# Moving batch 0's hand-over and the first two units' attention in among the last projections

## The reference

```
sa, ca, ga, sb, cb, gb = split(silu(c) @ wmod)         # per batch; ga, gb kept at least 0.25 from 0
h = layernorm(x) * (1 + ca) + sa
Q = elu(h Wq' + bq) + 1;  K = elu(h Wk' + bk) + 1;  V = h Wv' + bv
KV = sum over tokens of K (x) V, per head;  Ksum = sum over tokens of K
x = x + ga * ((Q KV / (Q . Ksum + 1e-6)) Wo' + bo)
h = layernorm(x) * (1 + cb) + sb
logits = cosine(h, centroids) + h . w_route;  gates = softmax over the two largest
x = x + gb * sum over experts of gate_e * (gelu(h w1_e + b1_e) w2_e + b2_e)
```

## Time and profile before

| | |
|---|---|
| median of 3 runs | 370.66 us |
| profiled execution | 370.4 us |
| its span | 368.6 us |
| TensorE matmul busy | 95% |
| VectorE, ScalarE, GpSimd busy | 80%, 63%, 71% |
| mean granted TensorE clock | 0.995 |

### The profile page before, as it was taken

The page is one execution under the profiler, slowest core; times in us unless marked ns, Lnnn a source line. Parts: engine busy times, 40 slices in busy tenths (PEclk is TensorE's granted clock), DMA queues, the critical chain, the costliest instruction groups (busy, mean ns, idle before and its releaser), DMA issues.

```text
span 368.6 us, 8941 instructions
## 1 busy us (share of the span) xinstructions
PE 348.6 (95%) x2762; PEld 324.9 (88%) x2762; DVE 294.4 (80%) x828; ACT 233.2 (63%) x510; POOL 263.2 (71%) x374
## 2 busy tenths in 40 slices
PE   7999999999997778699999999999999999999895
PEld 7877888888886677699999999999999999999895
DVE  4768777778776779989999898898988988887754
ACT  4476787787974475568384684674855856855541
POOL 3446999999886748887878889778778777666200
PEclk9999999999999899999999999999999999999999
DMA  7942630000000020341321323224214224224221
GB/s 271 331 143 66 202 108 0 0 0 2 1 2 0 2 93 31 110 126 56 109 86 60 129 59 105 88 70 131 86 58 142 79 65 130 94 68 138 83 69 57
DMA packets 23712, 31.78 MB, mean 86 GB/s; under 512 B 2288, under 2 KB 14204, under 8 KB 23680
## 3 DMA queue, kind: packets, MB, share of 16 engines
q1 hardware_dynamic: 23240, 31.34, 27.3%
q10 hardware_dynamic: 440, 0.04, 0.1%
HBM read 27.04 MB, written 4.34 MB: 85 GB/s over the span
## 4 chain that ended last, share of the span: by engine, by line
PE 78%; DVE 12%; issue 4%; ACT 3%; DMA 2%; POOL 1%; ACTq 0%; DVEq 0%; POOLq 0%
PE bank L777 22%; PE bank L779 20%; PE bank L778 20%; PE bank L785 5%; PE bank L844 2%; PE bank L815 2%; PE bank L956 2%; DMA g_bc<-in_b 1%; DVE hid_g L1357 1%; PE bank L882 1%; DVE den L1296 1%; PE bank L997 1%; DVE bank L1374 1%; PE bank L890 1%; DVE gT_f L1413 1%
## 5 line engine op out<-in xcount | busy, mean ns | idle before, releaser
L717 ACT ACTIVATE bank<-bank,cols_sb 128x256 f32<-128x256 f32 x128 | 51.3, 439 | 48.1 <-PE bank L779 47.7
L777 PE MATMUL bank<-tr_hi,w_hi 128*128 128x256 f32 x256 | 73.8, 288 | 0.0
L779 PE MATMUL bank<-tr_hi,w_lo 128*128 128x256 f32 x256 | 72.7, 284 | 0.0
L778 PE MATMUL bank<-tr_lo,w_hi 128*128 128x256 f32 x256 | 72.6, 283 | 0.0
L777 PE MATMUL bank<-w_hi,hid_pair 128*128 128x256 f32 x252 | 70.4, 280 | 0.1
L779 PE MATMUL bank<-w_hi,hid_pair 128*128 128x256 f32 x252 | 70.2, 279 | 0.0
L778 PE MATMUL bank<-w_lo,hid_pair 128*128 128x256 f32 x252 | 70.2, 278 | 0.0
L489 POOL TENSOR_TENSOR hid_pair<-hid_g,hid_pair 128x512 fp32r<-128x512 f32 x42 | 54.2, 1291 | 7.1 <-ACT hid_pair L724 3.9
L777 PEld LDWEIGHTS bank<-tr_hi,w_hi 128*128 128x128 f32 x256 | 48.9, 191 | 0.1
L779 PEld LDWEIGHTS bank<-tr_hi,w_lo 128*128 128x128 f32 x256 | 48.8, 191 | 0.0
L778 PEld LDWEIGHTS bank<-tr_lo,w_hi 128*128 128x128 f32 x256 | 48.8, 191 | 0.0
(11 more groups left out here) (159 smaller groups left out, 937.2 us busy)
## 6 DMA issues: line engine op xcount, KB each, us to landing
g_bc<-g_dram SPq DMA_DIRECT2D x64, 256.0 KB, 3.5
x_sb<-in_x SPq DMA_DIRECT2D x16, 256.0 KB, 3.3
out<-x_sb SPq DMA_DIRECT2D x15, 256.0 KB, 2.3
early<-in_wmod SPq DMA_DIRECT2D x3, 512.0 KB, 7.0
q_sb<-in_w SPq DMA_DIRECT2D x2, 512.0 KB, 6.4
q_sb<-in_w SPq DMA_DIRECT2D x1, 1024.0 KB, 9.4
mod_row<-mod_dram SPq DMA_DIRECT2D x1, 1024.0 KB, 6.2
q_sb<-in_wqkvT SPq DMA_DIRECT2D x2, 384.0 KB, 5.2
```

Source lines behind the costliest of these rows:

```text
L717: last = ac.activation(half, half, ACT.Gelu, bias=b1_sb[:, e:e + 1])
L777: te.matmul(out_ap, l_hi, r_hi, start=start, stop=False, skip_group_check=shared)
L778: te.matmul(out_ap, l_hi, r_lo, start=False, stop=False, skip_group_check=shared)
L779: return te.matmul(out_ap, l_lo, r_hi, start=False, stop=stop, skip_group_check=shared)
```

## The change

Batch 0's hand-over goes into steps 9 to 11 of phase A, the attention of units 0 and 1 and the norm of unit 0 into steps 10 to 15. The steps 8 to 15 are written out on all engines, and of the hand-written prologue only a few calls are left.

```diff
@@ TensorE, step_a
                 qk(u, 0)
+                if u.nth(NU - 1):
+                    attend(unit(1))
                 if u.plus(1) and not u.nth(0):
                     tp_a(u.plus(1))
+                if u.nth(UPB + 1):
+                    sum_k(0, bank[0][:, 0:E])
+                if u.nth(UPB + 2):
+                    make_m(0, bank[1])
+                if u.nth(UPB + 4):
+                    tp_o(unit(0))
+                if u.nth(UPB + 6):
+                    tp_o(unit(1))
                 qk(u, 1)
...
+                if u.nth(UPB + 5):
+                    attend(unit(0))
                 v(u)
@@ TensorE, step_e and what stands between the phases
+            def fill(to, n):
+                for _ in range(n):
+                    te.matmul(to[:, 0:E], ones_r[:, :], b2_r[:, :], start=True, stop=True)
...
+                if u.nth(1):
+                    first(u, 2)
                 if u.plus(3):
                     attend(u.plus(3))
-                if u and not u.nth(0):
+                if u and not early:
                     first(u, 2)
...
+                if u.nth(-1):
+                    pe.wait_ge(a_acc, NU + 1)
+                    fill(bank[6], 7)
                 if u.plus(2):
                     tp_e(u.plus(2))
+                if u.nth(-1):
+                    fill(bank[6], 11)
...
                     route(u.plus(2))
+                if u.nth(-1):
+                    sum_k(1, bank[6][:, 0:E])
+            pipeline(te, step_a, 2, 4, UPB)
+            tp_e(u0)
+            kv(unit(NU - 1))
             pe.wait_ge(route_ready, 1)
             route(u0)
@@ GpSimd, step_a (rstd_e(unit(0)) comes first in step UPB + 6)
+                if u.nth(UPB + 2):
+                    pool.wait_ge(f_ksrow, 1)
+                    gp.memset(prod[:, :, D:D + 1], DEN_EPS)
+                    make_prod(unit(0))
+                if u.nth(UPB + 3):
+                    make_qz(unit(0))
+                    make_prod(unit(1))
+                if u.nth(UPB + 4):
+                    make_qz(unit(1))
+                if u.nth(UPB + 6):
+                    make_prod(unit(2))
-                if u.plus(-2) and not u.plus(-2).nth(NU - 4) and not u.plus(-2).nth(NU - 3):
+                if u.plus(-2) and not any(u.nth(j) for j in range(UPB + 2, NU)):
                     add_bo(u.plus(-2))
@@ GpSimd, step_e
-                if any(u.nth(j) for j in range(2, 6)):
-                    add_bo(u.plus(NU - 6))
+                if u.plus(-2) and not any(u.nth(j) for j in range(UPB + 2, NU)):
+                    add_bo(u.plus(UPB - 2))
@@ ScalarE
+            def hi_m(b, product):
+                act.wait_ge(f_m_read, b + 1)
+                ac.activation(m_hi[:, b, :, :].rearrange("p c n -> p (c n)"), product[:, :], ACT.Copy).then_inc(f_m_hi, 1)
...
             def step_a(u):
+                if u.nth(UPB + 3):
+                    hi_m(0, bank[1])
                 negative_part(u, 0)
...
-                if u.plus(1) and cast_at_end(u.plus(1)):
+                if u.plus(1) and cast_late(u.plus(1)):
                     cast_activations(u.plus(1))
...
                 exp_qk(u, 1)
+                if u.nth(UPB + 6):
+                    normalise_e(unit(0))
+                if u.nth(UPB + 6):
+                    hi_o(unit(1))
                 if u.plus(2):
                     normalise(u.plus(2))
+                if u.nth(UPB + 4):
+                    hi_o(unit(0))
+                if u.nth(NU - 1):
+                    square(unit(0))
+                keep_v(u)
@@ VectorE, step_a, with mask_kv and split_m cut in two each (place_kv; scale_m and lo_m)
                 if u.plus(-2):
                     add_kv(u.plus(-2))
+                if u.nth(UPB + 3):
+                    denominators(unit(0))
+                if u.nth(UPB + 4):
+                    denominators(unit(1))
+                if u.nth(NU - 1):
+                    denominators(unit(2))
                 if not u.nth(0) and not u.nth(1):
                     split_weights(u)
...
                 feature_map(u, 0)
+                if u.nth(NU - 1):
+                    add_attention(unit(1))
                 feature_map(u, 1)
...
+                if u.nth(UPB + 1):
+                    keep_ksum(0, bank[0][:, 0:E])
+                    ve.memset(kv_m[:, :, :], 0.0)
+                    mask_kv(0)
+                    place_kv(0)
+                if u.nth(UPB + 2):
+                    scale_m(0, bank[1])
+                if u.nth(UPB + 3):
+                    lo_m(0, bank[1])
+                if u.nth(UPB + 4):
+                    lo_o(unit(0))
+                if u.nth(UPB + 5):
+                    add_attention(unit(0))
+                    stats_e(unit(0))
+                if u.nth(UPB + 6):
+                    lo_o(unit(1))
+                    modulate_e(unit(0))
+                if u.nth(NU - 1):
+                    stats_e(unit(1))
@@ VectorE, step_e (batch 1: place_kv in step 3 behind gates_b, scale_m at the end of step 3, lo_m in step 4)
-                if u.nth(-1):
-                    keep_ksum(1, bank[5][:, 0:E])
...
+                if u.nth(-1):
+                    keep_ksum(1, bank[6][:, 0:E])
```

More of the change, by code:

```diff
@@ L759, in step_e @@
                     hi_hid(u, 3)
-            pipeline(ac, step_a, 0, 2, NU - 4, NU - 1)
-            hi_o(u0)
-            step_a(unit(NU - 1))
-            hi_o(unit(1))
-            keep_v(unit(NU - 1))
-            normalise_e(u0)
-            square(u0)
+                if u.nth(3):
+                    hi_m(1, bank[7])
+            pipeline(ac, step_a, 0, 2, UPB)
             hi_e(u0)
@@ L791, in tp_a @@
                 wait(pe, a_xn, u.count(1, 1))
-                wait(pe, a_hf, u.count(1, -1))
-                if u.nth(NU - 2):
-                    pe.wait_ge(f_ksrow, 1)
-                if u.nth(NU - 1):
-                    pe.wait_ge(f_m_read, 1)
-                transposes(nat[:, u.h, :, :], bank[u.h]).then_inc(a_tp, 1)
+                wait(pe, a_hf, u.count(1, 0))
+                transposes(nat[:, 0, :, :], bank[5]).then_inc(a_tp, 1)
             def qk(u, t):
@@ L878, in _ @@
             for c in range(NC):
-                last = te.matmul(bank[5][:, 0:NE], ones_f, cent_sq[:, c, :], start=(c == 0), stop=(c == NC - 1))
+                last = te.matmul(bank[0][:, 0:NE], ones_f, cent_sq[:, c, :], start=(c == 0), stop=(c == NC - 1))
             last.then_inc(cent_done, 1)
@@ L911, in make_m @@
                 last.then_inc(f_m, 1)
-            pe.wait_ge(a_hf, NU - 3)
-            sum_k(0, bank[0][:, 0:E])
-            step_a(unit(NU - 3))
-            pe.wait_ge(d_wo, 16)
-            pe.wait_ge(a_hf, NU - 2)
-            make_m(0, bank[1])
             def tp_o(u):
@@ L946, in tp_e @@
                     wait(pe, o_x1, u.count(1, 2))
-                transposes(nat[:, u.h, :, :], bank[0]).then_inc(e_tp, 1)
+                transposes(nat[:, 1, :, :], bank[0]).then_inc(e_tp, 1)
             def route(u):
-                h = u.h
+                h = place_e(u)
                 wait(pe, e_lo, u.count(1, 1))
@@ L1058, in step_e @@
                     route(u.plus(2))
[L1060 to L1070 removed]
+                if u.nth(-1):
+                    sum_k(1, bank[6][:, 0:E])
+            pipeline(te, step_a, 2, 4, UPB)
+            tp_e(u0)
             kv(unit(NU - 1))
[L1072 to L1075 removed]
+            pe.wait_ge(b2_ready, 3)
             pe.wait_ge(route_ready, 1)
@@ L1475, in step_e @@
                 if u.nth(3):
-                    split_m(1, bank[7])
-            dve.wait_ge(mod_got, 16)
-            ve.memset(kv_m[:, :, :], 0.0)
-            keep_ksum(0, bank[0][:, 0:E])
-            mask_kv(0)
-            step_a(unit(NU - 3))
-            split_m(0, bank[1])
-            step_a(unit(NU - 2))
-            denominators(u0)
-            lo_o(u0)
-            denominators(unit(1))
-            add_kv(unit(NU - 3))
-            split_weights(unit(NU - 1))
-            dve.wait_ge(w_ready, NU)
@@ L1498, in _ @@
+            clip_centroids()
+            stats_a(unit(2))
+            split_b2()
+            split_route()
+            step_a(u0)
+            mod_rows(0)
+            bias_o()
+            step_a(unit(1))
+            mod_rows(1)
+            pipeline(ve, step_a, 2, 4, UPB)
             add_kv(unit(NU - 2))
-            modulate_e(u0)
-            add_attention(unit(1))
-            denominators(unit(2))
+            lo_e(u0)
             add_kv(unit(NU - 1))
-            lo_e(u0)
-            stats_e(unit(1))
```

278 lines of the change are left out of this document (118 added, 160 removed).

## The result

The kernel takes 367.06 us in the median after the change (366.38 to 369.39, 11 runs) and 370.58 us before it (367.74 to 371.76, 11 runs in turn with them): ratio 0.9922, 95% interval 0.9893 to 0.9951, so 3.5 us or 0.8% faster. The forecast was 367.0. The profiled execution took 367.11 us with a span of 365.0, the one before 370.4 with 368.6.

What follows compares the result with a forecast made beforehand. TensorE was taken as the bound, 95% busy, with VectorE late in the changeover. Terms -2.8 - 1.05 + 1.85 - 1.55 and 0.05 rounding gain 3.6 us: 366.8 from the profiled 370.4, 367.0 as median; range 363.7 to 371.0.

Steps and rivals of the forecast that it cites:

- Steps 8 to 14: End of the projections: seven steps of 41.5 us, plus 3.45 of added TensorE work and 1.45 of waits.
- The wait for split_lo(13): Step 12: GpSimd's added work makes TensorE wait 0.5 us for the low part of unit 13; bounds 0 and 1.3.
- ScalarE's 0.1: Steps 8 to 14: moving the activations' cast from VectorE to ScalarE costs 0.1 us; bounds 0 and 3.5 in all.
- make_m's wait as a cost: Step 10: TensorE waits 0.85 us at make_m(0) for VectorE's place_kv(0), counted in full; bounds 0 and 2.0.
- Step 15 to first(0,0): Changeover: 16.74 us becomes 10.55, 8.45 of work plus waits; a net gain of 2.8 us by first(0,0).
- The clock at first(0,0): Step -1: first(0,0) runs at the upper clock, of which VectorE takes 1.05 us; bounds 0 and 1.55.
- The new wait: End of step -1: keep_ksum(1) behind lo_e(1) waits for route(1) and sum_k(1), delaying VectorE's gates by 1.85 us.
- first(1,2): Steps 1 to 3: placed before attend(4), it fills 1.55 us of TensorE's 2.54 us wait there, counted as gain.
- place_kv(1) in step 3 instead of 2: VectorE's 0.59 us leaves step 2, bringing the gain to 3.6 us at lo_o(6), which ends the stop before 185.08.
- The rival in which steps 8 to 15 lengthen: Late projections: instructions in GpSimd's or VectorE's queue are paid in full by TensorE; 371.4 or 373 us; chance 0.18.
- Nothing kept: Later hand-over in steps 4 to 9 or lower clock, plus the new waits, takes back 3.6 us: 370.4; chance 0.07.
- the faster rival: The new wait costs nothing and the waits in steps 10 and 12 don't come: gain 6.9 us, 363.7; chance 0.17.

Runs made afterwards that it cites:

- second profile: The changed kernel unaltered, timed and profiled again beside the kernel before: 367.15 us, ratio 0.9911.

## Why the prediction was right, and where its terms were not

The time (367.0 against 367.06), the direction and the main mechanism (batch 0's hand-over hidden in the projections, paid back in part by one new wait) held. That the number fits to 0.1 us is luck in good part, in two ways. The span of the profiled pair shrank by the forecast 3.6 us, but 0.9 of that is the start; from qk(0,0)'s bias to the end the change brought 2.7 (3.0 by the second profile). And the split between schedule and clock came out the other way round: the prediction has 2.5 us of schedule (2.8 - 1.85 + 1.55) and 1.05 of clock, while at equal clock the executions show 1.2 us, and 2.3 come with the lower level. Of its signs, qk(15,0) came at 112.08 (112 to 113) and VectorE's chain from lo_e(1) to attend(4) grew by 1.6 us (1.5 to 2). First(0,0) came at 121.64 and not near 123, attend(4) waits 1.15 us and not 1 or less, and behind 182 us there is one small hole, 0.29 at 196.39. The terms, against the profiled executions:

- *Steps 8 to 14, 46.4 us.* Measured 46.46. make_m's wait for place_kv was taken at 0.85 and is 1.15, because the four masks took 1.98 us, not 1.41. The wait for split_lo(13), 0.5, and ScalarE's 0.1 didn't come: split_lo ends at 98.43 and qk(13,0) starts at 98.48, exactly at the edge. That the cover is this thin is shown by the two experiments that take it away: with add_bo back two steps are 2.3 us longer together, with VectorE's cast one is 0.74 longer.
- *make_m's wait as a cost.* It was put down at its size. It isn't worth it: moved away, 0.16 us came back, since GpSimd needs the time for its own low part (the 0.92 us before qk(11,0)).
- *Step 15 to first(0,0), 10.55 us.* Measured 9.56. The waits were 1.3 us too large in sum, the work 0.3 too small (8.45 against 8.74 busy). The wait before kv(15) is 0.73 (0.95), that for lo_o(1) doesn't exist (0.5), that for lo_e(0) is below 0.1 (0.65).
- *The clock at first(0,0), 1.05 us.* Measured 0.95 in the gap of the routes (11.70 against 12.65); taken alone in the kernel before, 1.40. The prediction spoke of that one low stretch and counted its absence once. It didn't see that attend(4)'s stop of 2.54 us is another place where the clock may fall, since the one profile had it at 1.00 there.
- *The new wait, 1.85 us.* Measured 1.61 between route(1) and route(2), in the change and alone in the kernel before (13.25 both times). The version that moves it away gets 1.3 of it back; 0.3 is the price of sum_k in its new place.
- *first(1,2), 1.55 us.* This is the term that was off the most: its mechanism failed. The stop before attend(4) falls as predicted, from 2.54 to 1.15, but TensorE gives the time back in front of tp_e(3) and of second(1,0) (0.33 and 0.57), because VectorE is the bound: route(3) gains no more than route(2). Alone in the kernel before it shortened the gap by 0.14. What the edit does bring is that the clock doesn't fall there: without it the change is 2.5 us slower, some 1.5 of them by the clock at that stop.
- *place_kv(1) in step 3 instead of 2, 0.6 us.* Measured 0.7 between route(4) and route(5) (16.15 us and not 16.83), where the stop before attend(6) falls to 0.65. The next step loses 0.3 of it at attend(7), where the prediction took TensorE as full. In the kernel before the stop before attend(6) was 1.42 us:

```profile
185.08 0.39 PE L777 MATMUL bank<-m_hi,qz_hi 128*128 128x256 f32 x1 [1.42 <-DVE qz_lo L1303]
```

- *The start*, 0.9 us earlier, was not in the forecast and is chance. That the single banks and the single nat buffer cost nothing was nearly right: up to qk(8,0) the changed kernel takes 0.3 us more, in step 6. Which of the changes ahead of step 8 does it wasn't tested.

Against the forecast the profiled pair gained 1.0 (step 15), 0.9 (start), 0.4 (from route(3) to route(6)) and 0.25 (new wait), and lost 1.5 (first(1,2)), 0.3 (units 0 to 7), 0.45 (behind route(6), 4.1 against 3.6, mostly matmuls that start 0.118 us apart and not 0.113) and 0.2 in the rest. So the sum was better than its parts.

The rival in which steps 8 to 15 lengthen fell: in the second profile steps 8 to 14 take 5.91, 6.35, 8.17, 5.91, 6.48, 7.28 and 6.34 us, and with 5.93 for a step and what TensorE was given in each, only step 10 is over by more than 0.1 us (1.46, of which 1.15 is the wait for the masks). Its reason was sound, though, and the change avoids it by moving add_bo: that kernel with add_bo back is at 370.04. Nothing kept fell as well. Of the faster rival one third held: the wait in step 12 didn't come, that in step 10 and the new one did.

Open: a low stretch costs 1.4 us where it was isolated at first(0,0), while executions of before with a mean clock of 0.995 have spans 2.5 us above those at 1.000. No profile of an execution at 1.000 of that kernel is there to say where the last microsecond is.

## What to carry to other kernels

Work that is moved beside a full engine is only free if the slack of the engines that feed it is made first: here 1.3 us of GpSimd a step had to go elsewhere, or all was lost. A wait that is seen on the bounding engine is worth at most what the next engine's lateness leaves, so look for what is late right behind it before you pay for its removal. And where TensorE stops for as long as it did here (2.5 us, or twice in a row) between full stretches, look at shortening the stop even when the schedule wins nothing: the clock behind it can be what is won, and it shows in the spread of the executions rather than in one profile. One stop alone may not be enough: in the kernel before, neither filling the one nor shortening the other gave a clear gain, and each left another long stop standing.

## What the runs showed of the hardware

- After the same stop of 2.54 us before the same matmuls TensorE's granted clock stayed at 1.00 in one execution (kernel before) and fell to 0.50, the level of 1.2 GHz, in another (the one with fillers before route(0)), for 3.4 us (15.66 us of window at 0.89 is 15.66 x 0.11 x 2). Two stops close together did the same: 0.83 and 1.50 us with route(0)'s transposes between them in the kernel before, 1.02 and 1.41 in the one with fillers, while 0.87 and 1.41 at the same place in the kernel before did not. In the two profiles of the changed kernel, with stops of 1.15 us at most, it did not fall behind any of them. By the Trainium skill (TensorE: Matmul & The Clock Gate, What's actually happening), "the default state is throttled, and activity releases the throttle"; the runs agree, with the addition that one profile doesn't tell whether a given stop will be followed by it.
- At the lower level, matmuls of 128x256 start 0.21 us apart and not 0.12, yet a low stretch cost between 0 us (at route(1)) and 1.5 us (at attend(4)), by whether TensorE was the bound there.
- At a granted clock of 1.00 the same matmuls of 128x256 without a wait between them start 0.113 us apart in some stretches and 0.118 in others: 361.50 to 364.22 in the kernel before against 357.82 to 360.65 in the changed one, 24 matmuls each. No run shows the reason, and over a stretch of 27 us it made 0.4 us.
- A mask on VectorE whose two inputs lie in SBUF took 0.285 us in the median of eight and 1.22 us at most. That one, the second of batch 0's four, went from 78.78 to 80.00, beside a 128x512 sum of GpSimd from 78.64 to 79.92. A second one, of batch 1's four, went from 174.24 to 175.44, beside GpSimd's make_prod from 174.07 to 175.36. By the Trainium skill (SBUF — State Buffer, 🔬 SBUF: two separate sides), a VectorE instruction with two SBUF inputs and one of GpSimd can't use the pair of ports they share together: the one that starts first keeps it for its whole length, and the other waits; the trace agrees.
- The time from the start of the span to the first projection differs by up to 1.35 us between executions of kernels that are alike up to there (16.63 to 17.98 us), over a third of what this change brought. Gaps between marks repeat within 0.1 us.
